# Expert loop of a fused two-layer kernel: four row tiles turned before the loop, results copied by ScalarE, stores of empty pairs skipped, half of the results' table zeroed beforehand

## The reference

```python
scores = softmax(logits)                       # [n tokens, E = 64]
_, topk_idx = top_k(logits + router_bias, 4)
topk_scores = take(scores, topk_idx); topk_scores /= topk_scores.sum(-1) + 1e-8
combine = zeros(n, E).at[arange(n)[:, None], topk_idx].add(topk_scores)
g = einsum('nd,edf->enf', flat, Wg); u = einsum('nd,edf->enf', flat, Wu)
hw = silu(g) * u * combine.T[:, :, None]
out = einsum('enf,efd->nd', hw, Wd)            # + the shared experts' rows
```

## Time and profile before

| | us |
|---|---|
| runs shown | 968.84 median of 3 (965.76 to 969.14) |
| profiled execution | 965.31, span 963.6 |
| busy: PE, DVE, ACT, POOL | 823.4, 673.9, 366.5, 326.8 |
| expert loop, first silu to last TensorE work | 372.2 to 532.1 |
| chain that ended last | PE 56%, DVE 23%, issue 6%, POOL 5%, ACT 5%, DMA 4% |

### The profile page before, as it was taken

How to read it: one execution, slowest core, us unless ns; L and a number is a source line. 1 busy time by engine, 2 the same in 40 slices (tenths; PEclk the granted TensorE clock), 3 DMA queues, 4 the chain that set the end, 5 groups by cost and what they waited for, 6 DMA issues and landing times.

```text
span 963.6 us, 18023 instructions
## 1 busy us (share of the span) xinstructions
PE 823.4 (85%) x6591; PEld 688.0 (71%) x6591; DVE 673.9 (70%) x1536; ACT 366.5 (38%) x732; POOL 326.8 (34%) x483
## 2 busy tenths in 40 slices
PE   5889989899878997777889059799999999999994
PEld 4667777777657886666678048688888888788883
DVE  5657766777358752898778166578898765867876
ACT  2244444444452363333112035445556654222220
POOL 3123232333433236675000471666664221100001
PEclk9899999999879999999999665878888978999998
DMA  7000000000000044898874532211110000000001
GB/s 262 1 2 13 13 2 12 13 13 13 13 11 1 23 129 140 263 290 270 252 236 150 169 90 73 66 45 33 49 54 28 0 1 1 0 1 23 22 1 44
DMA packets 49253, 67.96 MB, mean 71 GB/s; under 512 B 5912, under 2 KB 41880, under 8 KB 49176
## 3 DMA queue, kind: packets, MB, share of 16 engines
q1 hardware_dynamic: 24984, 31.28, 10.1%
q0 software_dynamic: 6784, 18.88, 6.7%
q10 hardware_dynamic: 17408, 16.78, 5.1%
HBM read 53.49 MB, written 23.07 MB: 79 GB/s over the span
## 4 chain that ended last, share of the span: by engine, by line
PE 56%; DVE 23%; issue 6%; POOL 5%; ACT 5%; DMA 4%; SPq 1%; POOLq 0%; DVEq 0%; ACTq 0%
PE S L1380 5%; PE ZO L1132 5%; PE ZO L1012 3%; PE S L1012 3%; PE S L1014 3%; PE S L1013 3%; PE S L997 3%; DVE st L1627 3%; PE S L1086 2%; PE ZO L1014 2%; PE ZO L1013 2%; PE ZO L1587 2%; DVE work L1635 2%; PE T L1587 2%; PE ZO L1391 1%
## 5 line engine op out<-in xcount | busy, mean ns | idle before, releaser
L502 POOL TENSOR_SCALAR veps<-mv 128x2 f32<-128x2 f32 (+1 forms) x63 | 15.4, 245 | 279.0 <-DVE mv L1630 278.8
L511 POOL TENSOR_SCALAR_AFFINE_SELECT work<-work 128x256 f32<-128x256 f32 x128 | 53.5, 442 | 120.4 <-ACT work L701 120.3
L1012 PE MATMUL ZO<-parts 128*128 128x256 f32 x224 | 71.6, 320 | 15.1 <-DVE parts L1669 6.5
L1012 PE MATMUL S<-xr,parts 128*128 128x512 f32 x192 | 82.9, 432 | 0.2 <-DVE work L1805 0.2
L581 POOL DMA_INDIRECT work<-xnd,rows_at x64 | 67.8, 1059 | 36.4 <-issue 17.7
L2114 DVE TENSOR_TENSOR work<-work,S 64x256 f32<-64x256 f32 x128 | 54.2, 424 | 35.2 <-ACT work L852 31.0
L1014 PE MATMUL S<-xr,parts 128*128 128x512 f32 x192 | 76.7, 399 | 0.0
L1013 PE MATMUL S<-xr,parts 128*128 128x512 f32 x192 | 76.3, 397 | 0.0
L701 ACT ACTIVATE work<-S 128x768 f32<-128x768 f32 x64 | 51.7, 812 | 54.7 <-PE S L1086 54.7
L1013 PE MATMUL ZO<-parts 128*128 128x256 f32 x224 | 66.3, 296 | 0.0
L1014 PE MATMUL ZO<-parts 128*128 128x256 f32 x224 | 66.0, 295 | 0.0
(11 more groups left out here) (348 smaller groups left out, 2307.8 us busy)
## 6 DMA issues: line engine op xcount, KB each, us to landing
yd<-work ACTq DMA_DIRECT2D x64, 256.0 KB, 3.2
raw<-in_experts SPq DMA_DIRECT2D x64, 192.0 KB
work<-in_experts SPq DMA_DIRECT2D x48, 192.0 KB
lg_all<-in_experts SPq DMA_DIRECT2D x16, 192.0 KB
xnd<-attn_w SPq DMA_DIRECT2D x8, 256.0 KB, 2.1
shd<-work SPq DMA_DIRECT2D x8, 256.0 KB, 2.4
raw<-in_ffn SPq DMA_DIRECT2D x2, 1024.0 KB, 5.6
x_sb<-in_x SPq DMA_DIRECT2D x1, 1792.0 KB, 8.8
```

The lines of the kernel that those rows point to most:

```text
L511: last = pool.affine_select(out=diagonal, in_=diagonal, compare_op=ALU.is_ge, fill=0.0, base=0, pattern=[[0, 2], [1, P]], channel_multipli ...
L1012: pe.matmul(dst, a(0), b(0), start=start, stop=False, skip_group_check=True)
```

## The change

- Tiles 0 to 3 are turned beside the last units of the shared part, all through bank S[3]; the loop begins with these four done. They wait for the gathers (`e_x`) and, one for one, for ScalarE's copy (`e_xc`).
- The result copy moves from VectorE to ScalarE, behind the store of pair i - 2 and ahead of the tiles' copies.
- A flag for each pair, 1 if it is empty, is computed by the router, turned and copied with the block table, and read by ScalarE into registers for eight pairs at a time. The store of a pair is conditional on it.
- The upper half of `yd` (64 blocks) is filled with zeros by eight stores of 1 MB during attention, from a zeroed stretch that is later `iotah`; VectorE waits for all eight (`y_zero`) before it writes `iotah`.
- VectorE's router steps are spread: one in every second pair up to 27, then one in every third.
- After the loop: GpSimd fills v1 and ones1 first; batch 0's gathers signal by place k, and VectorE sums place by place; the last layer's first weight loads wait until batch 0's last gathers have landed.

```diff
                 sp.dma_start(xnd[b * T:(b + 1) * T, :].rearrange("(t p) d -> p t d", p=P),
                              xn_all[:, 2 * b:2 * b + 2, :]).then_inc(s["x_st"], 16)
+                at = (XTILES + 8 * b) * P
+                sp.dma_start(yd[at:at + 8 * P, :].rearrange("(n p) d -> p n d", p=P),
+                             no_rows.unsqueeze(1).to_broadcast([P, 8, D])).then_inc(s["y_zero"], 16)
...
             for half in range(2):
-                sp.wait_ge(s["e_dn"], XPAIR)
                 if half:
                     sp.wait_ge(s["f_wl"], NSH + RING)
+                else:
+                    sp.wait_ge(s["e_dn"], XPAIR)
+                    sp.wait_ge(s["e_x3"], 32 * (XTP // RING) + 32)
...
+            pool.wait_ge(s["e_dn"], XPAIR)
+            pool.memset(v1, 1.0)
+            pool.memset(ones1, 1.0).then_inc(s["c_ones"], 1)
             for k in range(RING):
                 pool.wait_ge(s[f"e_o{k}"], 16 * (XPAIR // RING))
...
+            def expert_results(i):
+                act.wait_ge(s["e_dn"], i + 1)
+                if i >= RING:
+                    act.wait_ge(s[f"e_o{i % RING}"], 16 * (i // RING))
+                act.activation(ysb[:, i % RING].rearrange("p b h d -> p h b d"),
+                               (TT, ZO)[i % 2][:].rearrange("p (h x) -> p h x", h=2)[:, :, 0:2 * P]
+                               .rearrange("p h (b d) -> p h b d", b=2), ACT.Copy).then_inc(s["e_y"], 1)
...
                 act.dma_start(yd_places[chunk, turn, q].rearrange("b p d -> p b d"),
-                              ysb[:, i % RING].rearrange("p b h d -> p b (h d)")).then_inc(s[f"e_o{i % RING}"], 16)
+                              ysb[:, i % RING].rearrange("p b h d -> p b (h d)"),
+                              cond=idle[i % WRING] < 1).then_inc(s[f"e_o{i % RING}"], 16)
...
                     act.activation(sgx[64:128, i % 2, :], S[2 + i % 2][0:64, 0:256], ACT.Silu).then_inc(s["e_sg"], 1)
                     if i >= 2:
-                        expert_rows(i - 2)
+                        if (i - 2) % WRING == 0:
+                            idle = idle_in((i - 2) // WRING)
+                        expert_rows(i - 2, idle)
+                    if i:
+                        expert_results(i - 1)
...
+            for n in range(AHEAD + 1, NQ * NJ):
+                gate(n)
+                up(n)
+                if n >= AHEAD + 2:
+                    down_unit(n - 2)
+                    expert_transposes(n - AHEAD - 2)
+            down_unit(NQ * NJ - 2)
+            expert_transposes(2)
+            down_unit(NQ * NJ - 1)
+            expert_transposes(3)
...
+                dve.tensor_scalar(ebcol[:, 3:4], ebcol[:, 0:1], E - 0.5, None, ALU.is_ge)
...
+            dve.wait_ge(s["y_zero"], 16 * NB)
             dve.tensor_copy(iotah[:], bc(iota[:].unsqueeze(2), [P, P, TOPK]))
```

More of the change, by code:

```diff
@@ L89, in build @@
         iotah = sb("iotah", [P, P, TOPK], F16)
+        no_rows = iotah[:].rearrange("p a b -> p (a b)").bitcast(F32)
         topk16 = sb("topk16", [P, TOPK, NT], F16)
@@ L610, in shared_row, with first_gathers @@
                                ).then_inc(s["m_in1" if b % 2 else "m_in"], 16)
+            def first_gathers():
+                shared_row(0)
+                for k in range(TOPK):
+                    for t in range(2):
+                        pool.indirect_dma_start(gathered(0, t, k), None, yd[:],
+                                                bass.IndirectOffsetOnAxis(ap=slots[:, t, k:k + 1], axis=0)
+                                                ).then_inc(s[f"e_x{k}"], 16)
             def gathers(b):
-                if b == 0:
-                    shared_row(b)
                 gather_rows(b, range(2 * TOPK))
-                if b:
-                    shared_row(b)
+                shared_row(b)
             def denominators(b, cp):
@@ L632, in _ @@
             pool.wait_ge(s["r_w"], 1)
-            gathers(0)
+            first_gathers()
             pool.wait_ge(s["e_y"], XPAIR)
@@ L1360, in expert_transposes @@
                         o = (b * KC + c) * P
-                        last = pe.transpose(S[j % 2][:, o:o + P], xg[:, j % RING, b, c * P:(c + 1) * P], ident[:])
+                        last = pe.transpose(turn_bank(j)[:, o:o + P], xg[:, j % RING, b, c * P:(c + 1) * P], ident[:])
                 last.then_inc(s["e_xt"], 1)
@@ L1399, in _ @@
             pe.wait_ge(s["r_eb"], 1)
-            turned = 0
-            for i in range(-1, XPAIR):
+            turned = EARLY
+            for i in range(XPAIR):
                 if i >= 0:
@@ L2065, in second_constants, with beside_pair, first_sum @@
                     dve.tensor_copy(gA, bc(ident[:, 127:128], [P, T])).then_inc(s["c_const"], 1)
+            def beside_pair(i):
+                if i < 28:
+                    return (i - 1) // 2 if i % 2 else None
+                return 14 + (i - 28) // 3 if i % 3 == 1 else None
+            def first_sum(ch):
+                dve.wait_ge(s["m_in"], 16)
+                for k in range(TOPK):
+                    dve.wait_ge(s[f"e_x{k}"], 32 * (XTP // RING) + 32)
+                    for t in range(2):
+                        last = dve.scalar_tensor_tensor(sums(0)[:, t, :], gathered(0, t, k), wtop[:, t, k:k + 1],
+                                                        sums(0)[:, t, :], ALU.mult, ALU.add)
+                    ch(last)
+                dve.sem_inc(s["m_add"], 1)
             def moe_sum(b, ch, places=range(TOPK)):
-                dve.wait_ge(s["m_in1" if b % 2 else "m_in"], 16 * 9 * (b // 2 + 1))
+                dve.wait_ge(s["m_in1" if b % 2 else "m_in"], 16 * 9 * (b // 2 + 1) - (0 if b % 2 else 16 * 8))
                 for k in places:
@@ L2107, in _ @@
             dve.memset(xt_rows[:, XWORDS - KC * P:XWORDS], 0.0).then_inc(s["r_inv"], 1)
[L2108 to L2115, removed]
[L2116 to L2129 removed]
+            for i in range(XPAIR):
+                dve.wait_ge(s["e_sg"], i + 1)
+                if i >= 2:
+                    dve.wait_ge(s["e_dn"], i - 1)
+                for half in range(2):
+                    last = dve.tensor_tensor(hx[64 * half:64 * half + 64, i % 2, :], sgx[64:128, i % 2, :],
+                                             S[2 + i % 2][64:128, 0:256], ALU.mult)
+                last.then_inc(s["e_h"], 1)
+                k = beside_pair(i)
+                if k is not None and k < 16:
+                    weight_step(k)
+                elif k is not None and k < 22:
+                    padded_slots(k - 16)
+                elif k is not None and k < 25:
+                    second_constants(k - 22)
+            dve.wait_ge(s["e_dn"], XPAIR)
             second_constants(3)
[L2131 removed]
+            first_sum(ch)
             moe_stats(0, ch)
```

80 lines of the change are left out of this document (40 added, 40 removed).

## The result

The changed kernel's median is 955.91 us (949.3 to 962.01, 10 runs), beside 965.62 (961.5 to 971.96, 10 runs) for the kernel before; the ratio is 0.989, with a 95% interval from 0.9853 to 0.9926. That is 9.7 us faster, where 15.2 were summed up and 952.5 forecast. Its profiled execution took 958.3 us. Its span was 956.6, which is 7.0 less than the 963.6 of before.

The account below looks back on a forecast made before the run. VectorE was taken to hold the expert loop's first part; -4.7 - 4.7 + 0 + 1.3 - 7.1 = -15.2 on 965.3 gave 950.1, 953.6 with the median's offset. Forecast 952.5, range 944.5 to 961.

Parts of the forecast that it names:

- Early tiles, -4.7: Loop start: tiles turned early bring pair 3's silu from 385.84 to 381.1, a gain of 4.7 us.
- Pairs 3 to 27, -4.7: Expert loop's first part: 22.4 us per eight pairs, 67.2 against 71.9, a gain of 4.7 us.
- late by about another 0.6 every eight: Loop to pair 27: with faster pairs, weights not issuable before pair 11 is down come about 0.6 us later every eight.
- the 0.65 that the flags were to show: Loop to pair 27: ScalarE's flag read, taken as 0.98 us, shows 0.65 of it ahead of tile copies, three times.
- DMA holds the loop: Rival, chance 0.20: at DMA share 0.86 the loop gives nothing or 2 us; 958.5, with the offset 961.
- waits for weights grow by more than 5 us: Sign in the loop that the prediction is wrong: waits for weights grow by more than 5 us.
- The copy and the flags on ScalarE: Expert loop: ScalarE's work in a pair without tiles fits TensorE's 1.76 us with 0.2 to 0.3 to spare.
- the rival with 974: Rival, chance 0.07: ScalarE becomes the loop's pace, 21.6 us lost, 971.7 in total, with the median's offset 974.
- Pairs 28 to 63, 0: Loop's second part: about 0.8 us saved on VectorE and 0.8 lost to router steps; zero, bounds -3 and +4.
- Zeroed table, +1.3: End of attention: VectorE waits for the last 1 MB store before iotah; 1.3 us late, bounds 0 and 2.9.
- Behind the loop, -7.1: After the loop: GpSimd starts 6.4 us earlier and the layernorm step 0.7 more; 7.1 gained, bounds 5 and 8.
- Skipped stores inside the loop, 0: Pairs 28 to 63: skipped stores take traffic where TensorE, not DMA, sets the pace; nothing gained.

Follow-up runs that it names:

- e11: The kernel before with the four early tiles alone; copy on VectorE, all stores made, no zeroed table: 959.06 us, ratio 0.9912.
- e3: The kernel before with only the skipped stores, the zeroed table and the new order behind the loop: 960.01 us, ratio 0.994.
- e2: The changed kernel with the result copy back on VectorE and router steps in pairs 4 to 28 as before: 955.85 us, ratio 0.9895.
- e4: The changed kernel with loads for the next eight pairs issued ahead of the reloads on SP: 967.77 us, ratio 1.0018.
- e12: The changed kernel without expert weight loads from pair 12 on, for timing only: 943.69 us.
- e10: The changed kernel with the stores of all 64 pairs made, idle ones too: 955.5 us, ratio 0.9876.
- e9: The changed kernel with the late iotah write of e1 and the VectorE copy of e2 together: 953.55 us, ratio 0.9865.
- e5: The changed kernel without expert weight loads from pair 12 on, for timing only: 944.61 us in the execution not at half clock.
- e1: The changed kernel with VectorE's wait for the zeroed table and iotah write moved to the end of router step 1: 953.56 us, ratio 0.986.

## Why the prediction was nearly right, and where it was not

952.5 was forecast and 955.9 came. One term was wrong by itself, one undersized, three held. That the total came so near is in part luck. From the 968.84 of the runs shown, 952.5 meant 16.3 us less; 9.7 were measured, beside a kernel before that was 3.2 lower.

- *Early tiles, -4.7:* right. -3.9 in the changed kernel, -4.6 in e11, and GpSimd's fifth tile follows the fourth after 0.30 us. By medians they are worth 4.2 (e3 against e2) or 8.5 (e11). The stretch scatters too: pairs 0 to 3 took 11.73 in e3 without early tiles and 11.31 in e4 with them.
- *Pairs 3 to 27, -4.7:* wrong; it was +0.8, which is no change within the scatter of 2 us, and each eight pairs took 24.3 and not 22 to 23. VectorE's waits did go, from 7.0 to 0.4. The step that failed is the one on weights, "late by about another 0.6 every eight". That is 1.8 for the three eights, and the loads cost 7.2 there (e12 against the changed kernel). The step looked at pair 16, the first load of the next eight, and not at the reload of a place within the same eight, for which three pairs are all the time there is: 6.05 us without a wait, and the one at pair 14 landed 5.81 after an issue that itself came 0.8 after pair 10 was down. It also counted only the wait, and not the matmuls that ran at the lower clock behind it. The rest of that term was about right: without weights the sum is 21.8 x 3 = 65.4, and e12 took 65.5. Its smaller parts bear this out: TensorE's wait behind the second of the two pairs that turn two tiles grew from 0.97 to 1.48 and from 0.93 to 1.60, near the 0.65 that the flags were to show. It is the rival "DMA holds the loop", in the form of single late transfers. The earlier start, though, was not given back (e11). The mark "waits for weights grow by more than 5 us" was passed, with 5.7.
- *The copy and the flags on ScalarE:* ScalarE is not the pace in the last pairs: 0.78 of each 1.75 is idle, and the rival with 974 was far off.
- *Pairs 28 to 63, 0:* +1.1 was measured, within the 71.3 to 75.1 that the kernels with loads and the usual order of loads take there.
- *Zeroed table, +1.3:* undersized by 2.8 in the mean of all kernels and by 3.8 in this one. The store landed in 4.84, earlier than my 5.6. The Trainium skill's page "DMA: Bandwidth & Descriptors" (Anatomy of one DMA) gives 4.4 by a formula measured on DMAs that GpSimd issues; this store is issued by SP, and took 0.4 longer than that. VectorE waited 2.10, less than the 2.8 forecast, but the write behind it took 1.75 and not 0.43, so 1.8 were lost. What I left out is this slow write and TensorE, which ran dry for 2.59 us and then had half the clock for 10 us. The upper bound of 2.9 was too low too.
- *Behind the loop, -7.1:* right in size (-7.5), but not shown to be by the cause that I priced. I credited the skipped stores. e10 shows that 4.6 of the 6.5 us at GpSimd's start come without them; what they bring beside the moved loads is 1.85. The last store is late where the next weights are issued with it (before, e11) and not where they aren't (e10). I had seen this ("travel together") and then counted their move as a possible loss.
- *Skipped stores inside the loop, 0:* right; e10 is no slower, though DMA's share from 500 to 520 fell from 0.41 to 0.18.

What stays open: the loops of kernels that differ in nothing there (156.0 and 151.9 for e9 and e2) are 4 us apart, and why was not looked for, so the copy's place is only known to be worth less than that. TensorE's clock differs as well: between pairs 3 and 27 it was 0.93 to 1.00 in the kernels with loads, and TensorE was busy there for 55.8 to 59.0 us with the same work. That the reloads' lateness could be mended by more places or another queue was not tried; e4 shows only that it can be made worse.

## What to carry to other kernels

Before a unit is made faster, list each transfer in the loop with its two ends, what allows its issue and what needs it, and count the distance in iterations; the ones with the fewest are the first to set the loop's next pace, however far ahead the others run. An engine at 94% of a window may be the bound, and its relief still be worth nothing. When the last transfer of a stage is slow, look first at what was issued in the same microsecond: with that moved, 4.6 us were gained with all stores still made. And a short wait is to be priced with what it does to TensorE: 1.8 us on VectorE became 5 here, and 4 in the mean.

## What the runs showed of the hardware that I had not expected

One execution of e5 was granted about half the clock from the first slice to the last; its span was 1287.1 us, the next execution took 944.61. TensorE was busy for 95% of it. The page's slices:

```profile
PE   6999999999889999999995699999999999999997
...
PEclk8555555555555555555555555555555555555555
```

The write of `iotah` took 1.75 to 1.97 us where it follows the landing of the 1 MB store that had read the same buffer, and 0.43 elsewhere, in e1 as in before. So it was in all eight kernels with the wait. The write itself shows no wait in the profile; the cause was not looked for.
